# Second tile's transposes in one stretch, weights loaded behind the gathers (DLRM tower, one core)

## What is computed

```
e = stack([tbl_k[ids[:, k]] for k in range(26)], axis=1)          # 2048 x 26 x 128
c = concatenate([dense[:, None, :], e], axis=1)                   # 27 vectors
inter = einsum('bfd,bgd->bfg', c, c)[:, iu, ju]                   # 351 pairs
h = concatenate([dense, inter, dense], axis=1)                    # 607
h = maximum(h @ W_top1 + b_top1, 0)                               # 512
h = maximum(h @ W_top2 + b_top2, 0)                               # 256
y = h @ W_top3
```

## Time and profile before

| | us |
|---|---|
| median of 3 runs | 381.77 (381.22 to 381.79) |
| profiled execution | 382.01 |
| its span | 380.2 |
| PE busy | 341.6 (90%) |
| PE weight loads busy | 327.4 (86%) |
| DVE busy | 243.5 (64%) |
| ACT busy | 147.8 (39%) |
| POOL busy | 250.9 (66%) |

### The profile page before, as it was taken

How to read it: one execution, slowest core, us unless ns; L and a number is a source line. 1 busy time by engine, 2 the same in 40 slices (tenths; PEclk the granted TensorE clock), 3 DMA queues, 4 the chain that set the end, 5 groups by cost and what they waited for, 6 DMA issues and landing times.

```text
span 380.2 us, 15163 instructions
## 1 busy us (share of the span) xinstructions
PE 341.6 (90%) x6472; PEld 327.4 (86%) x6472; DVE 243.5 (64%) x308; ACT 147.8 (39%) x305; POOL 250.9 (66%) x265
## 2 busy tenths in 40 slices
PE   0478754999989999999999999999999999999996
PEld 0468644899979998999989998999989997999996
DVE  3779817499257946589267936598367926697133
ACT  2356422444325224434335224434334224523431
POOL 6788778767777777677766776767766776661000
PEclk9989888799999999999999999999999999999999
DMA  7978972333233332243232332333333422110000
GB/s 180 248 182 215 278 233 56 82 79 107 79 97 77 84 104 69 70 103 83 83 91 71 94 93 71 74 97 77 83 92 75 105 84 62 49 47 14 0 2 1
DMA packets 20607, 36.05 MB, mean 95 GB/s; under 512 B 7698, under 2 KB 9490, under 8 KB 20596
## 3 DMA queue, kind: packets, MB, share of 16 engines
q0 software_dynamic: 8192, 16.79, 18.1%
q1 hardware_dynamic: 12260, 18.84, 17.8%
q10 hardware_dynamic: 144, 0.26, 0.3%
HBM read 35.87 MB, written 0.01 MB: 94 GB/s over the span
## 4 chain that ended last, share of the span: by engine, by line
PE 83%; DMA 6%; issue 5%; DVE 2%; POOL 2%; ACT 1%; SPq 0%; DVEq 0%; POOLq 0%
PE oh_ps L671 39%; PE work_ps L697 14%; PE work_ps L744 11%; PE tr_ps L682 7%; PE work_ps L786 5%; DMA emb<-table,ids_sb 4%; PE work_ps L709 3%; POOL emb L313 2%; DVE onehot L523 1%; DMA gram<-table 1%; PE work_ps L726 1%; PE work_ps L718 1%; PE oh_ps L786 1%; PE work_ps L722 1%; PE work_ps L775 1%
## 5 line engine op out<-in xcount | busy, mean ns | idle before, releaser
L313 POOL DMA_INDIRECT emb<-table,ids_sb x256 | 250.0, 977 | 92.2 <-issue 70.5
L523 DVE TENSOR_TENSOR onehot<-ids_b,rows_ps 125x1024 fp32r<-125x1024 int32 (+1 forms) x160 | 189.7, 1239 | 28.5 <-PE oh_ps L671 23.4
L671 PE MATMUL oh_ps<-onehot,hi 125*128 125x256 f32 x656 | 167.8, 294 | 17.8 <-DVE lo L536 13.2
L671 PE MATMUL oh_ps<-onehot,lo 125*128 125x256 f32 x656 | 163.2, 287 | 0.0
L671 PEld LDWEIGHTS oh_ps<-onehot,hi 125*128 125x128 f32 x656 | 128.0, 195 | 20.8 <-issue 15.1
L671 PEld LDWEIGHTS oh_ps<-onehot,lo 125*128 125x128 f32 x656 | 128.4, 196 | 0.0
L374 ACT ACTIVATE emb_t<-oh_ps 128x256 f32<-128x256 f32 x80 | 51.2, 642 | 105.8 <-PE oh_ps L671 104.2
L697 PE MATMUL work_ps<-emb_t 128*32 128x26 f32 x4096 | 53.1, 197 | 9.5 <-issue 5.6
L697 PEld LDWEIGHTS work_ps<-emb_t 128*32 128x32 f32 x4096 | 45.8, 111 | 17.3 <-issue 14.3
L563 DVE SCALAR_TENSOR_TENSOR top_in<-work_ps,top_in 128x512 fp32r<-128x512 f32 x14 | 9.6, 687 | 56.3 <-ACT top_in L417 56.3
L390 ACT ACTIVATE emb_t<-tr_ps 128x512 f32<-128x512 f32 x64 | 43.4, 746 | 4.7 <-PE tr_ps L682 4.7
(11 more groups left out here) (108 smaller groups left out, 238.1 us busy)
## 6 DMA issues: line engine op xcount, KB each, us to landing
ids_b<-ids_t SPq DMA_DIRECT2D x39, 256.0 KB, 3.5
emb<-table,ids_sb POOLq DMA_INDIRECT x256, 2.6
emb_t<-table SPq DMA_DIRECT2D x3, 448.0 KB
dense_sb<-dense_t SPq DMA_DIRECT2D x8, 128.0 KB
emb<-table SPq DMA_DIRECT2D x2, 448.0 KB
gram<-table SPq DMA_DIRECT2D x2, 448.0 KB
pairs<-table SPq DMA_DIRECT2D x2, 448.0 KB
gram<-w SPq DMA_DIRECT2D x1, 768.0 KB, 4.6
```

The lines of the kernel that those rows point to most:

```text
L313: pool.indirect_dma_start(emb[:, i, s, :], None, tables[t], bass.IndirectOffsetOnAxis(ap=ids_sb[:, i, t:t + 1], axis=0),).then_inc(gathere ...
L523: dve.tensor_tensor(onehot[:, n % ONEHOT_BUFFERS, 0:h, :], ids_b[0:CHUNK_ROWS, u, :].unsqueeze(1).to_broadcast([CHUNK_ROWS, h, PAIR]), row ...
L671: mm = pe.matmul(oh_ps[u % 2][:, 0, :], part[:, CHUNK_BASE[u] + chunk, :], onehot[:, (HALVES * u + s) % ONEHOT_BUFFERS, c, :], start=chunk ...
```

## The change

Four edits.

1. **PE, second tile.** The transposes of tile 1 no longer stand in two pairs (behind unit 7 and behind unit 9) but all 16 behind unit 9, in the order of `SECOND_ORDER` (groups 3, 2, 0, 1). Groups 3 and 2 go to `work_ps[1]` and `work_ps[2]`, which stand free then, the others to `tr_ps` as before. ACT takes them in the same order. New waits go with it: the first of these groups waits for both low parts of the pairs, part 1 of the first layer for the first group moved, the first gram product for two groups moved.
2. **PE, first layer.** Both parts follow the transposes; part 0 no longer stands between units 8 and 9.
3. **POOL.** Group (1, 2) waits for the transposes of tile 0 of the same step, no longer for the first half of unit 3.
4. **SP.** All loads of weights are moved behind the end of the gathers of tile 1 of step 0, `w1_raw` first; the ids of the next step's first two tables come ahead of them, and the other ids of that step stay behind them.

```diff
+            sp.wait_ge(onehot_ready, 2 * HALVES)
+            spread_ids(1, 0)
+
+            for g in range(NG):
+                sp.wait_ge(gathered[1][g], 16 * GROUP)
+            sp.wait_ge(lo_made, ONE)
+            sp.dma_start(w1_raw, w1[D:D + 3 * P, :].rearrange("(k p) n -> p k n", p=P)).then_inc(w1_ready, 16)
             sp.dma_start(w1_dense, w1[0:D, :]).then_inc(w1_dense_ready, 16)
...
-                    pool.wait_ge(onehot_used, b * UNIT_HALVES + (HALVES * 3 + 1))
+                    pool.wait_ge(transposed, b * (2 * NG) + NG)
...
+                if i == 0 and g > 1:
+                    pe.wait_ge(slots_moved, b * (2 * NG) + (g - 1 + AHEAD))
+                if (i, g) == (1, SECOND_ORDER[0]):
+                    pe.wait_ge(pairs_lo_made, b * 2 + AHEAD)
                 for k, s in enumerate(GROUPS[g]):
-                    t = pe.transpose(tr_ps[g % 2][:, k, :], emb[:, i, s, :], ident[:, :])
+                    t = pe.transpose(slots_bank(i, g)[:, k, :], emb[:, i, s, :], ident[:, :])
...
                 if (i, u) == (0, 0):
                     pe.wait_ge(onehot_moved, b * ONE + (ONE + AHEAD))
+                    pe.wait_ge(slots_moved, b * (2 * NG) + (NG + 2 + AHEAD))
...
+                if f == 1:
+                    pe.wait_ge(slots_moved, b * (2 * NG) + (3 * NG + 1 + AHEAD))
...
                 unit(b, 7)
-                transposes(b, 1, 0)
-                transposes(b, 1, 1)
                 unit(b, 8)
+                unit(b, 9)
+                for g in SECOND_ORDER:
+                    transposes(b, 1, g)
                 with pe.If(b > 0):
-                    first(b - 1, 0)
-                unit(b, 9)
-                transposes(b, 1, 2)
-                transposes(b, 1, 3)
-                with pe.If(b > 0):
-                    first(b - 1, 1)
+                    for f in range(2):
+                        first(b - 1, f)
```

More of the change, by code:

```diff
@@ L44 @@
 NG = len(GROUPS)
+SECOND_ORDER = (3, 2, 0, 1)
 FIRST_ONEHOT = 1 + GATH
@@ L223, in turned_pairs, with slots_bank @@
             return work_ps[PAIR_BANK[f]][:, 0:n * PAIR].rearrange("k (j a q) -> k a j q", a=n, j=SHARE)
+        def slots_bank(i, g):
+            if i == 0 or g < 2:
+                return tr_ps[g % 2][:, :, :]
+            return work_ps[4 - g][:, :].rearrange("d (s p) -> d s p", s=GROUP)
         def h1_parts(f):
@@ L263, in _ @@
             load_dense(0)
+            sp.wait_ge(onehot_ready, 2 * HALVES)
[4 more added lines that the diff above has]
+            sp.dma_start(w1_raw, w1[D:D + 3 * P, :].rearrange("(k p) n -> p k n", p=P)).then_inc(w1_ready, 16)
             sp.dma_start(w1_dense, w1[0:D, :]).then_inc(w1_dense_ready, 16)
             sp.dma_start(w1_twice[:, :], w1[D + 3 * P:D + 3 * P + D, :]).then_inc(w1_dense_ready, 16)
+            sp.dma_start(w2_raw, w2.rearrange("(k p) n -> p k n", p=P)).then_inc(w2_ready, 16)
             sp.dma_start(b2_sb[:, :], b2.rearrange("(a n) -> a n", a=1).to_broadcast([P, H2])).then_inc(vectors_ready, 16)
@@ L268, in _ @@
               .then_inc(vectors_ready, 16)
[L270 to L274, removed]
             def next_loads(b):
@@ L388, in take_slots @@
             def take_slots(b, i, g):
-                act.wait_ge(transposed, b * (2 * NG) + (i * NG + g + 1))
+                act.wait_ge(transposed, b * (2 * NG) + (i * NG + (SECOND_ORDER.index(g) if i else g) + 1))
                 act.activation(emb_t[:, i, :, 1 + GROUP * g:1 + GROUP * (g + 1)],
-                               tr_ps[g % 2][:, :, :].rearrange("d f p -> d p f"), ACT.Copy).then_inc(slots_moved, 1)
+                               slots_bank(i, g).rearrange("d f p -> d p f"), ACT.Copy).then_inc(slots_moved, 1)
             def take_gram(b, i, u):
@@ L445, in _ @@
             dense_hi(0)
-            take_slots(0, 1, 0)
-            take_slots(0, 1, 1)
             take_onehot(0, 8)
             take_onehot(0, 9)
-            take_slots(0, 1, 2)
-            take_slots(0, 1, 3)
+            for g in SECOND_ORDER:
+                take_slots(0, 1, g)
             act.wait_ge(w1_ready, 16)
@@ L482, in _ @@
                 take_onehot(b, 7)
-                take_slots(b, 1, 0)
-                take_slots(b, 1, 1)
                 take_onehot(b, 8)
-                relu_hi(b - 1, 0)
                 take_onehot(b, 9)
-                take_slots(b, 1, 2)
-                take_slots(b, 1, 3)
-                relu_hi(b - 1, 1)
+                for g in SECOND_ORDER:
+                    take_slots(b, 1, g)
+                for f in range(2):
+                    relu_hi(b - 1, f)
                 dense_hi(b)
@@ L677, in transposes @@
                 pe.wait_ge(gathered[i][g], b * (16 * GROUP) + 16 * GROUP)
-                n = i * NG + g
-                if g > 1:
-                    pe.wait_ge(slots_moved, b * (2 * NG) + (n - 1 + AHEAD))
+                if i == 0 and g > 1:
+                    pe.wait_ge(slots_moved, b * (2 * NG) + (g - 1 + AHEAD))
+                if (i, g) == (1, SECOND_ORDER[0]):
+                    pe.wait_ge(pairs_lo_made, b * 2 + AHEAD)
                 for k, s in enumerate(GROUPS[g]):
-                    t = pe.transpose(tr_ps[g % 2][:, k, :], emb[:, i, s, :], ident[:, :])
+                    t = pe.transpose(slots_bank(i, g)[:, k, :], emb[:, i, s, :], ident[:, :])
                 t.then_inc(transposed, 1)
```

## The result

The change makes the kernel slower: 384.93 us (384.82 to 386.16, 4 runs) against 381.50 us (380.29 to 381.79, 4 runs) of the kernel before on the same chip, a ratio of 1.0099 with the 95% interval 1.0076 to 1.0123. The forecast was 378.9 us, and its range ended at 381.8. The profiled execution took 384.82 us with a span of 383.0 us, 2.8 us above the span before.

What follows compares the result with a forecast made beforehand. PE bounds steady steps, POOL's gathers price the gram. Step 2 starts 0.2 us late, five steps take 208.5 instead of 211.7 us, step 7 starts 2.9 us early: 382.01 becomes 379.1, or 378.9 against the runs' median; range 376.3 to 381.8.

Steps and rivals of the forecast that it cites:

- What bounds the kernel: Steady steps: PE's chain sets the 42.48 us step; POOL's gathers lengthen the gram by 0.47 us per us of cover.
- POOL's release: Steps 2 to 6: group (1,2) starts 1.45 us earlier, cover falls 5.96 to 4.5 us, gram 7.5 to 6.7 us.
- The line through three points: Gram against gather cover: no cover 4.6 us, 5.96 us cover 7.5, full cover 8.67; 0.47 us lost per us.
- PE's move, "I take 0": Moved transposes and first layer: merging changes under 0.1 us, DVE at unit 9 costs 0 to 0.2 us a step; taken as 0.
- the margin of 0.06 us at unit 9: DVE ends its one-hot halves at 222.24; unit 9's second half would start at 222.30 on PE.
- the DVE rival: Unit 9: DVE's halves come 0.4 us late in each of 7 steps, 2.8 us go, 381.7 us; chance 0.13.
- SP's weights: Step 0: gather wait gone, w1 not binding, gram 4.1 us early, code fetched under load; step 1 at 69.8 against 69.14.
- The next block takes 3.6 to 4.1 us as now: Step 0's gram: second and third code blocks take 3.6 to 4.1 us as before, or somewhat more.
- Code held up twice or more: Step 0's gram: two code blocks wait 10 us each, step 1 starts at 77.4, 385.5 us in all; chance 0.10.
- The rule that I weighed: DMA engines go round queue rows, changing at packet borders; load would cost code packets next to nothing, giving 377.0 us.
- the second case: Rival, code not held up: step 0's gram keeps 13.3 us, step 1 starts at 65.0, 377.0 us; chance 0.22.
- the forecast's three terms: Step 2 starts +0.2 us; five steps of 41.7 us take 208.5 instead of 211.7; nothing changes from step 7.

Runs made afterwards that it cites:

- pe_only: Kernel before with only PE's and ACT's new order, transposes and first layer behind unit 9: 384.69 us, ratio 1.0097 to the kernel before.
- pool_only: Kernel before with POOL's edit alone, group (1,2) waiting for the transposes of tile 0: 379.66 us, ratio 0.9976 to the kernel before.
- tr_before9: Kernel after with the 16 transposes ahead of unit 9 instead of behind it: 386.40 us, ratio 1.0117 to the kernel before.
- after_old_sp: Kernel after with the loads of weights where they stood before: 382.90 us, ratio 1.0057 to the kernel before.
- sp_only: Kernel before with SP's edit alone, all weights and ids behind the gathers of tile 1: 383.84 us, ratio 1.0085 to the kernel before.
- late_little: Kernel after with most weights left out behind the gathers, 0.4 MB and the ids remaining: 381.43 us, ratio 0.9998 to the kernel before.
- after_filler: Kernel after with eight extra transposes keeping PE busy between units 7 and 8 of step 0: 385.09 us, ratio 1.0103 to the kernel before.
- pool_w2_late_2: Kernel before with POOL's edit, w2_raw and ids behind the gathers of tile 1 of step 0: 378.49 us, ratio 0.9932 to the kernel before.

## Why the prediction was wrong, point by point

- **What bounds the kernel: right.** PE's chain sets the steady steps, and the gram is priced by the gathers beside it.
- **POOL's release: right in mechanism, a little too large.** Group (1,2) starts where forecast. Cover fell to 5.05 us in one step (last gather at 195.96, gram from 192.16) and 4.09 us in the next, 4.57 on average for the forecast 4.5; these grams took 7.10 and 6.76 us, 6.93 on average for the forecast 6.7 (6.8 over steps 2 to 6, where before had 7.4). The line through three points is too low at this end: from the earlier trace rows to here it is (7.51 - 6.93)/(5.96 - 4.57) = 0.42 us lost per us of cover, not 0.47. Over steps 2 to 6 the grams gained 2.85 us for the forecast 3.15. But part of it is not the release: steps that DVE lengthens leave less of the gram covered, which is worth 0.9 us in pe_only. In pool_only and in tr_before9, where DVE costs nothing, the grams gained 2.2 and 2.4 us. So the release itself was put too high by 0.7 to 0.9 us, and that the total came within 0.3 us is luck.
- **PE's move, "I take 0": wrong, the second cause of the miss.** The step that failed is the margin of 0.06 us at unit 9. It set the end of DVE's busy time against PE's start and left out the hand-over and the refill behind it (0.39 for 0.28 us, at both halves), and DVE started its halves 0.08 us later in the step than before. It cost 0.34 us in each of steps 2 to 6, 0.3 in step 7 and 0.6 in step 1, where PE waits for DVE all through: 2.6 us on the way to the grams. This was the DVE rival, at 0.13 with 0.4 us; its mechanism and the size per step hold (pe_only and after_old_sp show it, tr_before9 takes it away). Its net price is lower than the rival's 2.8 us, because the grams give part of it back: over steps 2 to 6 it is 1.1 us by tr_before9, of 1.5 on the way to the grams.
- **SP's weights: gathers right, code mis-sized, the first cause of the miss.** PE no longer waited for gathers, and w1 did not bind. The first block came on time by luck: working back from 69.8 the forecast took it up at 60.4, and it came at 60.58. Two errors cancel there. The forecast asks for the block at 52.1 and gives it 8.3 us. It was asked for near 54.4 (27 products into the gram, counted as in the forecast) and took 6.2 us, 3.6 to its packet and 2.6 more. The step that failed is "The next block takes 3.6 to 4.1 us as now (63.84 - 59.72, 67.41 - 63.84), or somewhat more, and so the third", of which the sum took the lower reading: they took 5.75 us (66.33 - 60.58) and 4.84 us (71.17 - 66.33), 2.9 us more than the 4.1 and 3.6 taken. I had reckoned 12 us for the load and then not applied it past the first block; the DMA engines are full until 64 us, and the second block's packet passes between 63.5 and 64. That is step 1's start: 69.8 + 0.2 + 2.9 = 72.9. The rival "Code held up twice or more" had the kind, but put 10 us on each block. sp_only, late_little and after_old_sp show that it is this load, and not the new order or the clock, that makes the stops long.
- **The clock in step 0: not seen.** The gram began at 54.0, not at 51.7. Eight transposes left the gap between units 7 and 8, DVE was late there, and PE came out of 3.7 us of idleness at 1.2 GHz. By after_filler it is worth 1.4 us at the gram's start, and the first block moves with it: taken up at 59.19 there instead of 60.58, with step 1 1.9 us earlier. It does not show as an error of the sum because the forecast's 8.3 us for that block were too long by 2.1.
- **The rule that I weighed.** The first stop grows from 1.35 to 1.59 us without load to 3.45 to 6.75 us with 2.3 to 3 MB, and the packet behind which PE goes on passes at 58 us instead of 56.75, although the gram began 1.8 us earlier. The instruction queue (packets, MB, share of 16 engines) in the half microsecond from 56.5 us of before, and from 58.0 and 63.5 us of after:

```profile
q8 instruction: 1, 0.02, 19.0%
```

```profile
q8 instruction: 1, 0.02, 15.7%
```

```profile
q8 instruction: 1, 0.02, 14.7%
```

PE takes the block up 2 to 3 us behind its packet in both kernels (59.72 and 60.58, 66.33). So the delay lies ahead of the packet, where the load is. From taking up one block to the packet of the next it is 1.5 us before (59.72 to 61.25) and 3.2 us after (60.58 to 63.75), with the packets placed to a quarter of a microsecond. The Trainium skill, page "DMA: Bandwidth & Descriptors", on queues, rings and completion order, has each DMA engine go round its queue rows and switch at packet borders. What fell is the forecast's reading that by this rule the load costs the code next to nothing, and with it the second case. Whether 1.7 us more is one packet of each other row, or the rule fails, no run here shows, nor which part of the request waits.

Added up: the forecast's three terms were +0.2 at step 2's start, -3.15 for steps 2 to 6, nothing behind: -2.9. Measured: +3.7, -1.2, +0.3: +2.8. Of the difference of 5.7 us, 3.1 arise in step 0 (2.9 of them at the second and third code block), 0.6, 1.7 and 0.3 are DVE at unit 9 in step 1, in steps 2 to 6 and in step 7, and 0.3 are the grams' slightly smaller gain; step 1's gram was 0.2 us shorter than forecast.

## What to carry to other kernels

A load that is moved out of the way of one transfer lands on the next one: list what is read for the first time just behind it, code included, and follow the load until it has drained, not only to the first user. A margin of a few hundredths of a microsecond between a producer's busy end and a consumer's start is no margin: count the hand-over and the refill, at every half. And try the edits of a bundle one by one. POOL's wait with 1.0 to 1.5 MB of load behind the gathers gives 379.0 and 378.5 us (ratios 0.9942 and 0.9932), the fastest kernels here.

## What the runs showed of the hardware

- In step 0's gram, PE's first pass over code cost 1.35 to 2.5 us at each block of 256 instructions with no load behind the gathers. With 2.3 to 3 MB it cost 3.1 to 6.75 us at the first two blocks and 1.7 to 2.8 us at the third. The Trainium skill, page "Runtime: NRT & Kernel Launch", section "Instruction fetch mechanics", has blocks of 256 instructions fetched by a DMA queue, which the trace agrees with (127 or 128 products between two stops, and a packet on the instruction queue ahead of each block), and the cost of a border "mostly hidden". In this stretch of short matmuls it is not: three borders took 5.9 us before and 10.9 after.
- In step 0 the granted clock fell to 0.50, the 1.2 GHz level, around idle times ahead of unit 8 of 3.71 us (after), 3.83 (pe_only), 3.82 (late_little) and 2.85 (pool_w2_late_2), where unit 8's first matmul already took 0.58 us. After 3.00 and 3.05 us (sp_only, tr_before9) the first matmul still took 0.39 us, and the clock fell within unit 8, to 0.50 from 46 and 47 us on. After 2.54 and 2.48 us (after_filler, after_old_sp) it stayed at 1.00 through units 8 and 9. The length of the idle time alone does not order the cases: in before the clock fell to 0.50 within unit 7 (41 to 44 us), after idle times of 0.93 and 1.58 us. Each case is one trace, and what does order them stays open.
- One chip ran the kernel before and three of its variants at 500 to 512 us, with PE in issue at places where no new code is read (no packet on the instruction queue from 250 to 310 us). I have no cause for it.
